# Local attention's score sums: two streamed columns a product in place of 128

## The chip, the cores and the metric

The kernel runs on one core of one Trainium2 chip. The metric is the device time of one execution in microseconds (us); lower is better. The time before is the median of three runs.

## The reference

Two blocks of a small transformer run over `x` of 8 sequences (B) by 256 tokens (T) by 128 features. The change touches only the first stage of the first block, a local attention with 16 heads of 64 features, in which each token looks at four keys: one made from the conditioning vector of its sequence, and those of the token before it, of itself and of the token after it.

```python
q = (x @ WQ_w + WQ_b).reshape(Bx, Lx, nh, d)
k = (x @ WK_w + WK_b).reshape(Bx, Lx, nh, d)
ak = (ax @ WK_w + WK_b).reshape(Bx, 1, nh, d)
av = (ax @ WV_w + WV_b).reshape(Bx, 1, nh, d)
...
K = jnp.concatenate([akb, k_shift], axis=3)
V = jnp.concatenate([avb, k_shift], axis=3)
scores = jnp.einsum('blhd,blhjd->blhj', q, K) / jnp.sqrt(jnp.float32(d))
alphas = jax.nn.softmax(scores, axis=-1)
att = jnp.einsum('blhj,blhjd->blhd', alphas, V).reshape(Bx, Lx, nh * d)
return att @ WO_w + WO_b
```

After it come a linear attention, a recurrent scan with a routed feed-forward layer, a second scan with a differential attention, and a top-2 mixture of experts. They are not changed.

## The kernel before

`program` runs its stages one after the other, each in a `Block` of its own, and the next one's instructions start only when all engines have left the block before. `local_attention` is the second stage, after the small `setup`.

Features lie on the 128 partitions, tokens in the free dimension. A chunk `c` of 128 features is two heads, so there are 8 chunks; the 2048 tokens are cut into two halves of 1024. One half and one chunk is a unit `u`, and there are 16. For each unit:

- `project(u, i)` (TensorE, L280) makes queries and keys in five pieces: two of 512 query columns, two of 512 key columns, and one of 8. ScalarE (`keep_projections`, L367 and L370) copies each into `qb` and `kb`.
- `products(u)` (VectorE, L434 and L437) multiplies the query with each of the four keys, element by element, into `prod`: four operations of 128 x 1024.
- `scores(u, i)` (TensorE, L292) sums these products over the 64 features of each head. For token block `i` of 128 tokens (eight in a unit, `HB`) and key `j` (four, `J`), the 128 x 128 tile of `prod` is the stationary operand and a selector `headsel` is the streamed one. `headsel` has two columns that are not zero, ones in the first 64 partitions and ones in the last 64. All 32 sums of a unit are one accumulation group over the whole 128-column tile `sc`: a window of `headsel` is shifted so that its two columns of ones fall on columns `2k` and `2k + 1`, and the other 126 columns add zero.
- `softmax(u)` (VectorE, L447 to L472, with one exponential on ScalarE) reads the 64 used columns of `sc` and splits the probabilities into three bf16 parts; `turn_probs` (TensorE, L303) turns them over, ScalarE copies them (`keep_turned`, L381).
- `spread_probs(u, i)` (TensorE, L314) spreads each probability over the 64 features of its head, eight tiles of 512 columns; `terms` (VectorE, L482 and L486) multiplies each with its value into `term`, and `attended` (L493 and L497) adds them up to `att`.
- `project_out` (TensorE, L322) multiplies with the output weights and accumulates over chunks.

The order on each engine is written out by hand. In turn `u` of the main loop TensorE issues `scores(u + 1, 0)`, then seven times `scores(u + 1, i + 1)` followed by `spread_probs(u, i)`, and then `project(u + 3, 0)`, the eighth `spread_probs`, `project(u + 3, 1)`, `project_out(u - 1, 1)`, the three key pieces, `project_out(u, 0)` and `turn_probs(u + 1)`. VectorE issues `products(u + 2)`, `attended(u - 1, 1)`, six `terms`, `softmax(u + 1)`, `attended(u, 0)` and two `terms`. `bc`, the target of a spread, has two buffers, so a spread waits for the term two before it. In the last three turns there is nothing left to project.

In fp32 one `nc.tensor.matmul` of the program is two pairs of a weight load and a matmul in the trace, so the 512 score sums are 1024 pairs, 64 for a unit.

Of the kernel before, what the change touches and what calls it, by code (L numbers as in the profile page):

```python
# [33 lines left out]
P = 128  # L34
# [3 lines left out]
HEADS, HD = 16, 64  # L38
# [133 lines left out]
def local_attention(nc, n, a, yB, wq, wk, wv, wo, wqkv, wout):  # L172

    HALF = TOK // 2
    HB = HALF // P
# [3 lines left out]
    J = 4  # L179
    with ExitStack() as local:  # L180
        def sb(name, shape, dt=F32):
            return local.enter_context(nc.sbuf_tensor(name, shape, dt))
# [5 lines left out]

        headsel = sb("headsel", [P, 2 * P])
        pick = sb("pick", [24, J, 2, HD], BF16)
        akT, avT = sb("akT", [P, NC, B]), sb("avT", [P, NC, B])
        qb = [sb(f"qb{i}", [P, HALF]) for i in range(4)]
# [1 line left out]
        prod = [sb(f"prod{i}", [P, J, HALF]) for i in range(2)]  # L196
# [10 lines left out]
        sc = local.enter_context(nc.psum_tensor("sc", [P, P // (2 * J), J, 2], F32))  # L207
# [13 lines left out]
        def pieces(u):  # L221
            h, c = divmod(u, NC)
            t0 = h * HALF
            k0 = 0 if h == 0 else t0 - SH
            return ([("q", t0, 0, 512), ("q", t0 + 512, 512, 512)]
                    + [("k", k0, SH, 512), ("k", k0 + 512, SH + 512, 512), ("k", k0 + 1024, SH + 1024, SH)])
# [6 lines left out]
        with nc.Block() as block:  # L233

            @block.sync
            def _(sp):
                sp.dma_start(wqkv[:, :], a["L0_attn_Wqkv"]).then_inc(n.load_linear, 16)
                sp.dma_start(wout[:, :, :], a["L0_attn_Wout"].rearrange("(c p) d -> p c d", p=P)).then_inc(n.load_linear, 16)
                for i, key in enumerate(("L0_cond2_W_ir", "L0_cond2_W_iz", "L0_cond2_W_in",
                                         "L0_cond2_W_hr", "L0_cond2_W_hz", "L0_cond2_W_hn")):  # L240
                    sp.dma_start(n.gru_w[:, i, :], a[key]).then_inc(n.load_later, 16)
                for i, key in enumerate(("L0_cond2_b_hn", "L0_cond2_b_ir", "L0_cond2_b_iz", "L0_cond2_b_in")):
                    sp.dma_start(n.gru_b[:, i, :], a[key].rearrange("(r d) -> r d", r=1)).then_inc(n.load_later, 16)
                sp.dma_start(n.b_l1[:, :], a["L1_cond_b"].rearrange("(r d) -> r d", r=1)).then_inc(n.load_later, 16)
                for dst, key in ((n.l1w, "L1_cond_W"), (n.wq12, "L1_attn_w_q12"), (n.wk12, "L1_attn_w_k12"),
                                 (n.wv1, "L1_attn_w_v"), (n.wmod, "L1_cond2_weight"), (n.b2, "L0_ffn_b2")):
                    sp.dma_start(dst[:, :], a[key]).then_inc(n.load_later, 16)
# [10 lines left out]
            @block.tensor  # L258
            def _(pe):
                pe.wait_ge(n.load_local, 64)  # L260

                for i, w in enumerate((wk, wv)):
                    for c in range(NC):
                        mm = nc.tensor.matmul(pj[i][:, B * c:B * c + B], w[:, P * c:P * c + P], n.condT,
                                              start=True, stop=True)
                    mm.then_inc(cond_proj, 1)
                pe.wait_ge(cond_kept, 2)
                pe.wait_ge(const_done, 2)
                pe.wait_ge(const_a, 4)

                def project(u, i):
                    if u >= UNITS:
                        return
                    c = u % NC
                    kind, src, _, width = pieces(u)[i]
                    w = wq if kind == "q" else wk
                    g = 5 * u + i
                    if g >= 2:
                        pe.wait_ge(proj_kept, g - 1)
                    nc.tensor.matmul(pj[g % 2][:, 0:width], w[:, P * c:P * c + P], n.xT[:, src:src + width],  # L280
                                     start=True, stop=True).then_inc(proj_done, 1)

                def scores(u, i):
                    if u >= UNITS:
                        return
                    if u >= 1 and i == 0:
                        pe.wait_ge(soft, 9 * u - 7)
                    if i == 0:
                        pe.wait_ge(prod_v, 4 * (u + 1))
                    for j in range(J):  # L290
                        k = J * i + j
                        mm = nc.tensor.matmul(sc[:, :, :, :].rearrange("p i j h -> p (i j h)"),  # L292
                                              prod[u % 2][:, j, P * i:P * i + P], headsel[:, P - 2 * k:2 * P - 2 * k],
                                              start=(k == 0), stop=(k == HB * J - 1))
                    if i == HB - 1:
                        mm.then_inc(score_done, 1)

                def turn_probs(u):
                    pe.wait_ge(parts_done, u + 1)
                    if u >= 1:  # L300
                        pe.wait_ge(turned_kept, u)
                    for i in range(HB):
                        mm = nc.tensor.transpose(tr[:, P * i:P * i + P],  # L303
                                                 parts[u % 2][:, i, :, :].rearrange("p k r -> p (k r)"), n.identb[:, :])
                    mm.then_inc(turned, 1)

                def spread_probs(u, i):
                    if i == 0:
                        pe.wait_ge(turned_kept, u + 1)
                    m, j = divmod(i, J)  # L310
                    g = 2 * J * u + i
                    if g >= 2:
                        pe.wait_ge(term_done, g - 1)
                    nc.tensor.matmul(bc[g % 2][:, :], pick[:, j, :, :].rearrange("r h d -> r (h d)"),  # L314
                                     probT[u % 2][:, 512 * m:512 * m + 512], start=True, stop=True).then_inc(spread, 1)

                def project_out(u, m):
                    h, c = divmod(u, NC)
                    if c == 0 and h == 1:
                        pe.wait_ge(y_kept, m + 1)  # L320
                    pe.wait_ge(att_done, 2 * u + m + 1)
                    nc.tensor.matmul(y_ps[m][:, :], wo[:, c, :], att[m][:, :], start=(c == 0),  # L322
                                     stop=(c == NC - 1)).then_inc(y_part, 1)

                for u in range(2):
                    for i in range(5):
                        project(u, i)
                for i in range(HB):
                    scores(0, i)
                for i in range(5):  # L330
                    project(2, i)
                turn_probs(0)


                for u in range(UNITS):
                    scores(u + 1, 0)
                    for i in range(HB - 1):
                        scores(u + 1, i + 1)
                        spread_probs(u, i)
                    project(u + 3, 0)  # L340
                    spread_probs(u, HB - 1)
                    project(u + 3, 1)
                    if u >= 1:
                        project_out(u - 1, 1)
                    for i in range(2, 5):
                        project(u + 3, i)
                    project_out(u, 0)
                    if u + 1 < UNITS:
                        turn_probs(u + 1)
                project_out(UNITS - 1, 1)  # L350
# [57 lines left out]
            def _(dve):  # L408
# [2 lines left out]
                nc.vector.memset(headsel[:, :], 0.0).then_inc(const_done, 1)  # L411
                dve.wait_ge(const_done, 1)
                for h in range(2):
                    nc.vector.memset(headsel[HD * h:HD * h + HD, P + h:P + h + 1], 1.0)

                for i in range(4):
                    nc.vector.memset(kb[i][:, 0:SH], 0.0)
# [1762 lines left out]
def program(nc, a, out):  # L2180
    with ExitStack() as ctx:
        n = allocate(nc, ctx)
        with ExitStack() as mid:
            yB = mid.enter_context(nc.sbuf_tensor("yB", [P, TOK], F32))
            wqkv = mid.enter_context(nc.sbuf_tensor("wqkv", [P, 3 * INNER], F32))
            wout = mid.enter_context(nc.sbuf_tensor("wout", [P, NC, D], F32))
            with ExitStack() as early:
                wq, wk, wv = (early.enter_context(nc.sbuf_tensor(k, [P, INNER], F32)) for k in ("wq", "wk", "wv"))
                wo = early.enter_context(nc.sbuf_tensor("wo", [P, NC, D], F32))
                setup(nc, n, a, wq, wk, wv, wo)  # L2190
                local_attention(nc, n, a, yB, wq, wk, wv, wo, wqkv, wout)
            linear_attention(nc, n, yB, wqkv, wout)
# [38 lines left out]
```

## Time and profile before

| | |
|---|---|
| three runs | 1698.83, 1699.10, 1703.48 us; median 1699.1 us |
| profiled execution | 1703.39 us in all, of which the span from the first instruction to the last is 1701.6 us |
| busy share over the span | TensorE 92%, VectorE 49%, ScalarE 39%, GpSimd 6% |
| granted TensorE clock, mean | 0.942 of full speed |
| local attention with `setup` | from 0 to about 371 us of the span |

Times inside the profile count from the start of the span. The profiled execution is 4.3 us longer than the median of the three runs, so a difference that is worked out inside it is added to both. The granted clock is given as a share of 2.4 GHz: 1.00 is that, and 0.50 is the other level, 1.2 GHz.

### The profile page before, as it was taken

The numbers are of one execution on the slowest core, as the hardware profiler recorded it, in microseconds if no ns is written. First come the engines' busy times: TensorE is split into PE (matmuls) and PEld (weight loads), VectorE is DVE, ScalarE is ACT, GpSimd is POOL, SyncE is SP. The second block draws the span as 40 slices with busy tenths as digits, with TensorE's granted clock in tenths as the row PEclk, the third lists the DMA queues.
The fourth block names the chain that finished last, engine by engine and source line by source line (L and its number), as shares of the span: only waits on it lengthen the run. The fifth ranks groups of instructions, "written<-read, shape, count | busy, mean of one in ns | idle before, by whom it ended". The sixth has DMA issues, their size and how long they took to land. (4 is left out here: it accounts for less than half of the span.)

```text
span 1701.6 us, 32009 instructions
## 1 busy us (share of the span) xinstructions
PE 1564.6 (92%) x11861; PEld 1250.0 (73%) x11862; DVE 827.5 (49%) x2926; ACT 662.9 (39%) x2449; POOL 94.7 (6%) x135
## 2 busy tenths in 40 slices
PE   7999989879999899999999999879999999866995
PEld 5666555537777799999999999638888888753663
DVE  2777668755445334444444444473333333565223
ACT  3211112125555145555555455314344434523442
POOL 0000000000000000000000000010000000003662
PEclk9988889889999999999999999859999999967998
DMA  4000000000000300000000000010000000001113
GB/s 146 1 1 1 0 1 1 1 0 1 1 1 1 100 1 2 2 1 2 2 2 1 2 2 1 1 31 21 20 26 20 27 14 2 1 1 47 41 43 92
DMA packets 27731, 28.05 MB, mean 16 GB/s; under 512 B 2293, under 2 KB 22234, under 8 KB 27450
## 3 DMA queue, kind: packets, MB, share of 16 engines
q1 hardware_dynamic: 20970, 16.70, 3.4%
q0 software_dynamic: 2496, 5.12, 1.0%
q10 hardware_dynamic: 4112, 4.19, 0.8%
q8 instruction: 96, 1.57, 0.4%
q14 instruction: 57, 0.47, 0.1%
HBM read 21.35 MB, written 4.65 MB: 15 GB/s over the span
## 5 line engine op out<-in xcount | busy, mean ns | idle before, releaser
L1457 PE MATMUL spare<-identb 128*128 128x128 bf16 x3166 | 218.2, 219 | 0.0
L1457 PEld LDWEIGHTS spare<-identb 128*128 128x128 bf16 x3166 | 201.7, 103 | 4.3
L292 PE MATMUL sc<-headsel,prod 128*128 128x128 f32 x1024 | 164.6, 315 | 0.7 <-DVE prod L437 0.7
L292 PEld LDWEIGHTS sc<-headsel,prod 128*128 128x128 f32 x1024 | 142.6, 218 | 26.7 <-issue 24.3
L1055 DVE TENSOR_TENSOR_SCAN narg<-rz,pre_n 128x16 f32<-128x16 f32 x256 | 47.9, 187 | 219.9 <-PE pre_n L952 218.9
L990 ACT ACTIVATE ghid<-gh_ps,cols 128x128 f32<-128x128 f32 x512 | 144.3, 366 | 12.9 <-PE gh_ps L891 12.7
L891 PE MATMUL gh_ps<-hist,w 128*128 128x128 f32 x1024 | 137.5, 275 | 0.6 <-ACT ghid L990 0.6
L900 PE MATMUL gy_ps<-w2e,ghid 128*128 128x128 f32 x1024 | 136.8, 276 | 0.6
L900 PEld LDWEIGHTS gy_ps<-w2e,ghid 128*128 128x128 f32 x1024 | 124.4, 191 | 3.0 <-issue 3.0
L891 PEld LDWEIGHTS gh_ps<-hist,w 128*128 128x128 f32 x1024 | 126.0, 188 | 0.8 <-DVE hist L1063 0.8
L952 PE MATMUL pre_r<-hist,gru_w 128*128 128x128 f32 x512 | 118.1, 312 | 0.7 <-DVE hist L1063 0.5
L1508 DVE TENSOR_TENSOR_SCAN targ<-gates,pairs 128x16 f32<-128x16 f32 x256 | 49.1, 192 | 141.4 <-ACT gates L1467 141.4
L976 ACT ACTIVATE rz<-pre_r 128x8 f32<-128x8 f32 x256 | 45.5, 178 | 182.6 <-PE pre_r L952 179.9
L1427 PEld LDWEIGHTS s_pre<-s,wT 128*128 128x128 f32 x512 | 76.9, 189 | 41.6 <-ACT s L1470 41.0
L1427 PE MATMUL s_pre<-s,wT 128*128 128x8 f32 x512 | 97.9, 263 | 2.9 <-ACT s L1470 1.1
L952 PE MATMUL pre_z<-hist,gru_w 128*128 128x128 f32 x512 | 100.0, 276 | 0.0
L952 PE MATMUL pre_n<-hist,gru_w 128*128 128x128 f32 x512 | 99.8, 276 | 0.0
L1505 DVE TENSOR_SCALAR pairs<-s,leak 128x8 f32<-128x8 f32 x256 | 59.6, 233 | 70.7 <-ACT s L1470 70.5
L952 PEld LDWEIGHTS pre_r<-hist,gru_w 128*128 128x128 f32 x512 | 77.1, 190 | 15.8 <-DVE hist L1063 1.0
L1467 ACT ACTIVATE gates<-s_pre 128x8 f32<-128x8 f32 x256 | 45.5, 178 | 108.0 <-PE s_pre L1427 108.0
L1470 ACT ACTIVATE s<-targ 128x8 f32<-128x8 f32 x256 | 53.4, 209 | 84.7 <-DVE targ L1508 84.7
L486 DVE TENSOR_TENSOR term<-bc,kb 128x512 f32<-128x512 f32 x96 | 63.3, 686 | 34.6 <-PE bc L314 34.4
(374 smaller groups left out, 2664.1 us busy)
## 6 DMA issues: line engine op xcount, KB each, us to landing
w<-in_L_ffn_W SPq DMA_DIRECT2D x1, 2048.0 KB, 9.6
raw<-in_L_ffn_wg SPq DMA_DIRECT2D x8, 256.0 KB, 2.9
raw<-in_L_ffn_wu SPq DMA_DIRECT2D x8, 256.0 KB, 2.8
raw<-in_L_ffn_wd SPq DMA_DIRECT2D x8, 256.0 KB, 2.7
wqkv<-in_L_attn_Wqkv SPq DMA_DIRECT2D x1, 1536.0 KB, 6.4
mrow<-mt SPq DMA_DIRECT2D x4, 256.0 KB, 2.4
y_top<-yrow SPq DMA_DIRECT2D x4, 256.0 KB, 5.4
y_next<-yrow ACTq DMA_DIRECT2D x4, 256.0 KB, 6.1
```

Source lines behind the costliest of these rows:

```text
L292: mm = nc.tensor.matmul(sc[:, :, :, :].rearrange("p i j h -> p (i j h)"), prod[u % 2][:, j, P * i:P * i + P], headsel[:, P - 2 * k:2 * P - ...
L486: nc.vector.tensor_tensor(term[s % 2][:, j, :], bc[g % 2][:, :], key(u, j, 512 * m, 512), ALU.mult).then_inc(term_done, 1)
L891: mm = nc.tensor.matmul(h_ps[:, f, :], w1[:, e, P * f:P * f + P], tokens(g), start=True, stop=True)
L900: mm = nc.tensor.matmul(y_ps, hid[v % 2][:, f, :], w2[:, e, f, :], start=(f == 0), stop=(f == NF - 1))
L952: nc.tensor.matmul(out, n.gru_w[:, i, :], h, start=False, stop=True, skip_group_check=True).then_inc(ready, 1)
L990: nc.scalar.activation(hid[v % 2][:, f, :], h_ps[:, f, :], ACT.Relu, bias=n.cols[:, at:at + 1]).then_inc(h_done, 1)
L1055: V.tensor_tensor_scan(narg[p][:, :], rz[p][:, 0:16], n_slot(s), 0.0, ALU.mult, ALU.add).then_inc(narg_done, 1)
L1427: nc.tensor.matmul(pre[s // G % 2][:, at:at + B], wT[:, 0, :], s2[:, 8 * s:8 * s + B], start=False, stop=True, skip_group_check=True).then ...
L1457: nc.tensor.matmul(spare[:, 0:P], n.identb[:, :], n.identb[:, :], start=True, stop=True)
L1470: nc.scalar.activation(s2[:, 8 * s + 8:8 * s + 16], second(targ[s % 2][:, :]), ACT.Tanh).then_inc(state, 1)
L1505: nc.vector.tensor_scalar(second(pair), s2[:, 8 * s:8 * s + 8], leak[:, 0:1], None, ALU.mult).then_inc(leaked, 1)
L1508: nc.vector.tensor_tensor_scan(targ[s % 2][:, :], gates[s % 2][:, :], pair, 0.0, ALU.mult, ALU.add).then_inc(arg_done, 1)
```

## The change

Each score sum becomes a matmul of its own. It streams two columns and writes two columns of `sc`, and it starts and stops its accumulation itself. The selector shrinks to two columns. The weight loads, their number and their order, the waits and the semaphores stay as they are.

```diff
-        headsel = sb("headsel", [P, 2 * P])
+        headsel = sb("headsel", [P, 2])
...
                     for j in range(J):
-                        k = J * i + j
-                        mm = nc.tensor.matmul(sc[:, :, :, :].rearrange("p i j h -> p (i j h)"),
-                                              prod[u % 2][:, j, P * i:P * i + P], headsel[:, P - 2 * k:2 * P - 2 * k],
-                                              start=(k == 0), stop=(k == HB * J - 1))
+                        mm = nc.tensor.matmul(sc[:, i, j, :], prod[u % 2][:, j, P * i:P * i + P], headsel[:, :],
+                                              start=True, stop=True)
                     if i == HB - 1:
                         mm.then_inc(score_done, 1)
...
                 for h in range(2):
-                    nc.vector.memset(headsel[HD * h:HD * h + HD, P + h:P + h + 1], 1.0)
+                    nc.vector.memset(headsel[HD * h:HD * h + HD, h:h + 1], 1.0)
```

## Rows read from the trace of the kernel before

**Rows 1.** The profile's page, second part: granted clock in 40 slices of the span

```profile
PEclk9988889889999999999999999859999999967998
```

**Rows 2.** The page's costliest groups: the score sums

```profile
L292 PE MATMUL sc<-headsel,prod 128*128 128x128 f32 x1024 | 164.6, 315 | 0.7 <-DVE prod L437 0.7
```

**Rows 3.** Timeline, turn 11: start, us, engine, what; in brackets idle before

```profile
278.14 1.22 DVE L434 TENSOR_TENSOR prod<-qb,akT 128x1024 f32<-128x1024 f32 x1 [0.29 <-ACT kb L370]
...
278.97 2.05 PE L292 MATMUL sc<-headsel,prod 128*128 128x128 f32 x16
...
285.29 0.38 PE L314 MATMUL bc<-probT,pick 24*128 24x512 bf16 x1 [1.46 <-DVE term L482]
...
286.70 0.39 PE L314 MATMUL bc<-probT,pick 24*128 24x512 bf16 x1
...
290.91 0.39 PE L314 MATMUL bc<-probT,pick 24*128 24x512 bf16 x1
...
297.22 1.22 DVE L434 TENSOR_TENSOR prod<-qb,akT 128x1024 f32<-128x1024 f32 x1 [0.29 <-ACT kb L370]
```

**Rows 4.** Timeline, ScalarE, just after the starts of turns 0, 13 and 14

```profile
43.79 1.01 ACT L381 ACTIVATE probT<-tr 24x1024 bf16<-24x1024 bf16 x1
...
317.23 1.01 ACT L381 ACTIVATE probT<-tr 24x1024 bf16<-24x1024 bf16 x1 [0.97 <-PE tr L303]
...
338.55 1.01 ACT L381 ACTIVATE probT<-tr 24x1024 bf16<-24x1024 bf16 x1 [7.06 <-PE tr L303]
```

**Rows 5.** Windows: length, busy us (count) of PE, PEld, DVE, ACT, POOL, PE clock, DMA share, GB/s

```profile
154.00:160.00 6.00, 6.00 (x24) 4.68 (x24) 1.70 (x3) 0.00 (x0) 0.00 (x0) 0.50 0.00 0
...
280.00:300.00 20.00, 18.54 (x104) 11.92 (x102) 16.46 (x28) 4.26 (x8) 0.00 (x0) 1.00 0.00 1
```

**Rows 6.** Timeline, TensorE: turns 5, 13 and 14

```profile
155.51 0.60 PE L314 MATMUL bc<-probT,pick 24*128 24x512 bf16 x1
...
158.05 0.60 PE L314 MATMUL bc<-probT,pick 24*128 24x512 bf16 x1
...
330.61 0.60 PE L314 MATMUL bc<-probT,pick 24*128 24x512 bf16 x2
...
338.44 3.39 PE L292 MATMUL sc<-headsel,prod 128*128 128x128 f32 x16
```

**Rows 7.** Timeline, the stretch up to 40 us

```profile
16.74 3.53 PEld L264 LDWEIGHTS pj<-cols,wv 128*128 128x128 f32 x16
...
20.82 3.47 PE L280 MATMUL pj<-xT,wq 128*128 128x512 f32 x4 [0.45 <-DVE avT L424]
...
31.86 7.22 PEld L292 LDWEIGHTS sc<-headsel,prod 128*128 128x128 f32 x64 [0.80 <-DVE prod L437]
...
39.01 0.30 PEld L280 LDWEIGHTS pj<-xT,wq 128*128 128x128 f32 x2
```

**Rows 8.** Timeline, last stage: router products of 8 columns, then transposes of 128

```profile
1524.13 5.49 PEld L1845 LDWEIGHTS bank_a<-cols,mB 128*128 128x128 f32 x32 [2.10 <-DVE mB L1992]
...
1529.36 1.76 PEld L1836 LDWEIGHTS xt_ps<-ident,mB 128*128 128x128 f32 x8
```

**Rows 9.** Windows of the same stage, columns as in Rows 5

```profile
1516.40:1522.00 5.60, 5.59 (x7) 2.50 (x8) 4.05 (x7) 0.00 (x0) 1.11 (x9) 0.50 0.01 1
...
1524.10:1525.50 1.40, 1.37 (x13) 1.37 (x13) 0.00 (x0) 0.00 (x0) 0.00 (x0) 1.00 0.00 0
1526.00:1529.30 3.30, 3.30 (x17) 3.30 (x17) 0.00 (x0) 0.00 (x0) 0.00 (x0) 0.50 0.00 0
1529.40:1532.40 3.00, 3.00 (x15) 2.63 (x16) 2.37 (x9) 1.20 (x2) 0.00 (x0) 0.50 0.04 11
1533.00:1534.00 1.00, 0.00 (x1) 0.00 (x0) 0.96 (x4) 0.98 (x3) 0.00 (x0) 1.00 1.07 286
```

**Rows 10.** Timeline, routing stage: eight bf16 products that stream one column

```profile
1102.37 0.29 PEld L1235 LDWEIGHTS r_sums<-r_ones,r_gt 128*128 128x128 bf16 x8 [0.73 <-DVE r_gt L1279]
...
1102.59 0.10 PEld L1238 LDWEIGHTS r_sums<-r_zeros,r_ones 128*128 128x128 bf16 x1
```

## The prediction

> **What bounds the kernel now.** I read the page's slices first, then the costliest groups, then the timeline of one turn of local attention, then the windows for the granted clock. The stages run one after the other, so what local attention gains or loses goes into the total one to one. Its score sums are the second largest group of the page: 1024 matmuls, mean 315 ns [rows 2]. The slices show that the clock is not at full speed in this stage: it is at 8 tenths in several of the first slices [rows 1].
>
> In the timeline of turn 11, which ran wholly at full clock, a turn lasts 297.22 - 278.14 = 19.08 us, and neither engine bounds it alone [rows 3]. VectorE starts its four products at 278.14; TensorE starts 16 pairs of score sums at 278.97, and at the third spread it stands for 1.46 us, until VectorE has released a `bc` buffer. That spread goes at 285.29, 6.32 us after the first score sum, and this interval is VectorE's. From there to the seventh spread at 290.91 TensorE sets the pace: four groups of one spread and eight score pairs, 1.41 us each. Then come query pieces, the last spread, output products, key pieces, and with them the copies that VectorE's next products wait for. So only four of a turn's eight groups of score pairs lie on the path that sets its length.
>
> The other thing to see is the clock. From the start of turn 0 to the start of turn 13 it takes 317.23 - 43.79 = 273.4 us [rows 4], 21.0 us for each of 13 turns, and not 19.08. The missing 25 us are stretches at half clock, like 154 to 160 us, in which the granted clock is 0.50 though TensorE is busy throughout [rows 5]. In such a stretch a group takes 158.05 - 155.51 = 2.54 us in place of 1.41, and 16 pairs take 3.39 us [rows 6].
>
> **The change part by part.** *The selector.* A memset becomes smaller, before VectorE's wait for the first projections. Nothing on the path: 0.
>
> *The streaming of 126 columns that add zero.* What does a pair cost now, and after? At full clock 64 pairs take 39.01 - 31.86 = 7.15 us, 112 ns each [rows 7]. A pair is a load of a 128 x 128 fp32 tile and a matmul, and loads overlap with matmuls. The nearest rows for a narrow product are the router's: the same fp32 tile as stationary operand, eight columns streamed. At granted clock 1.00 there are 13 of them in the window's 1.37 busy us, 105 ns each [rows 9]; at half clock 17 in 3.30 us, 194 ns, against 3.39 / 16 = 212 ns for the wide pair [rows 6, 9]. Windows count a cut instruction too, so these are low ends; all 32 take 1529.36 - 1524.13 = 5.23 us [rows 8], which is 13 at 112 ns and 19 at 199 ns. The start of the kernel has 16 more narrow pairs in 3.53 us, 220 ns each, at half speed by the next row, where a matmul of 512 columns takes 3.47 / 4 = 0.87 us [rows 7]. So the load sets a pair's time, narrow or wide, and the change takes next to nothing from it. The other end is the cheapest narrow product of the trace: eight bf16 ones of one column in 1102.59 - 1102.37 = 0.22 us, 28 ns each [rows 10]. Their stationary tile is bf16; the fp32 rows are nearer, and I take a saving of nothing per pair. What is saved is the end of each group, where the last wide product still streams while the spread behind it is loaded: at most one matmul, 0.1 us at full clock and 0.2 at half. I take half of that: a group at half clock costs 2.45 us, not 2.54.
>
> The Trainium skill has two rules here ("TensorE: Matmul & The Clock Gate"). "Back-to-back issue gap" makes the time fall with the streamed columns, to some 25 ns for a few of them; by this alone 64 pairs would shrink from 7.2 to an estimated 1.6 us. "LDWEIGHTS (loading the stationary operand)" makes the load go with the 128 columns of the stationary tile, an estimated 107 ns, and by this nothing is saved. The fp32 rows side with the second.
>
> *What the clock does.* This is the term that decides. In the last stage the clock is at 1.00 when the router's narrow products begin at 1524.13; it is still 1.00 up to 1525.5 and 0.50 from 1526 on, with TensorE and its weight loads busy for 3.30 of 3.30 us, and it stays there until 128-column transposes have run for over 3 us [rows 8, 9]. At the start of the kernel over 3 us of the same kind of product leave the speed at half as well [rows 7]. Weight loads and narrow products do not hold the clock in these rows. After the change the score sums are such products, and they fill most of the time from a turn's start to its seventh spread. Already now the clock is lost for a while in some turns, with wide products [rows 4, 5]. I expect it to fall in each turn's score part, and to come back in the part with the 512-column projections.
>
> *A turn after the change.* Score part: at the start the clock may still be full. If it falls 1.6 to 3.3 us in, TensorE has lost what the 1.46 us wait used to hold, and the third spread still goes about when VectorE releases it, at 6.32 us. Four groups at half clock follow: 4 x 2.45 = 9.8 us, against 5.6 now. The score part is 16.1 us in place of 290.91 - 278.97 = 11.9. Projection part: the turn's other 19.08 - 11.9 = 7.1 us of TensorE work at full clock. How long it runs at half, I bound by two rows: the transposes needed over 3.0 us, and 512-column products 5.6 us or a little more [rows 9]. I take the middle, 4.6 us, in which it does 2.3 us of its work: 9.4 us. A turn is 16.1 + 9.4 = 25.5 us.
>
> *The sum.* Turns 0 to 12: 13 x 25.5 = 331.5 us against 273.4: +58. Turn 13 has no projections: its score part was 330.61 - 317.12 = 13.5 us (its first score sum comes 0.11 us before the copy of rows 4) and becomes 16.1: +3. Turn 14 already begins at half clock, with 16 pairs in 3.39 us [rows 6], and is not held up by VectorE's products; its six groups go from 1.41 to 2.45 us: +6. The 64 pairs of unit 0, at 31.86, have full clock for some 3 us and then 0.21 us a pair in place of 0.112 [rows 6, 7]: 11 us against 7.15, and 2 more before the clock is back: +6. Together +73. The profiled execution would take 1703.4 + 73 = 1776 us, and the median 1699.1 + 73 = 1772 us.
>
> **The rivals.**
>
> *The clock holds (faster, 10%).* If weight loads count as work, TensorE is as busy as before and the clock behaves as now, or better. For it: TensorE's row is busy throughout, and the window from 280 to 300 us has the present pattern at 1.00 [rows 5]. Against it: 3.30 us of unbroken loads at 0.50 [rows 9]. Then only the group ends are saved: 0.1 us x 4 groups x 16 turns = 6 us at most, and should the present half-clock stretches vanish too, another 25. I price it at 1693, at best 1668. It decides if the clock stays at 1.00 in the score part for more than about 8 of 13 turns. The Trainium skill supports it ("TensorE: Matmul & The Clock Gate", "HAM oscillation"): it lays the loss of the clock to idle gaps of TensorE, and the change adds none. By that rule the time would be the 1693 above; the router's rows disagree.
>
> *The pair gets cheap (faster, 4%).* If a narrow fp32 pair cost 28 ns, TensorE would no longer bound even at half clock, and VectorE would: it is busy 16.46 of 20 us [rows 5], so 15.7 of 19.08, and with its wait for ScalarE a turn would be some 16.5. 13 x (21.0 - 16.5) = 58 us less: 1641. The router's 32 narrow pairs in 5.23 us speak against it.
>
> *The clock stays down (slower still, 12%).* If the projections of a turn do not bring the clock back before the next score part, all is at half: 3.4 + 6 x 2.45 = 18.1 us up to the seventh spread, and 7.1 us of TensorE work, most of which doubles, some 13: 31 us a turn, 13 x 10 = 130 more, with the 15 of the other turns 1844. Against it: clocks came back in 3 to 6 us of dense streaming, and the projection part at half clock lasts twice that.
>
> *Half as bad (slower, 6%).* The clock falls in about half of the turns, or late in each: half of the 73 us, 1736.
>
> **How the numbers follow.** The forecast, that the clock falls in each score part and comes back in each projection part, gets 68%. Its own range: with 3.2 us at half in the projections and groups of 2.35 us a turn is 24.4 us, 1756; with 5.9 us at half and a clock that falls after 1.6 us, so that the third spread is 1 us late, 27.2 us, and 1798. The range for all reaches from the half-bad case to the lower part of the all-half case: 1732 to 1840. It leaves out the two faster rivals, 14%, and about half of the all-half one. A measurement of this kernel tells about 0.3%, 5 us, from no change. Faster by more than that: 11% (both faster rivals, less the part in which only a few us are saved). Within 0.3%: 3%. Slower: 86%.
>
> **What the profile after would show.** The granted clock of 20 to 375 us at 0.6 to 0.75; it falls in the score part and rises in the key pieces of nearly every turn. Starts of turns some 25.5 us apart. No 1.46 us wait at the third spread, or a short one. 64 pairs of unit 0 still over 7 us. Stages after local attention the same length. The prediction is wrong if score pairs come at under 80 ns, or if the clock stays at 1.00 through score parts.

## The result, and the profile after

The changed kernel takes 1776.9 us (median of four runs, 1776.35 to 1777.74) against 1699.0 us before: slower by a factor of 1.0461, 95% interval 1.0428 to 1.0494. The forecast was 1772 us. The profiled execution took 1776.35 us, its span 1774.6 us.

From the page of the kernel after, the clock slices and the two groups of the score sums, to be held against [rows 1, 2]:

```profile
PEclk7666566565999999999999999967999999976998
...
L291 PEld LDWEIGHTS sc<-headsel,prod 128*128 128x128 f32 x1024 | 190.5, 281 | 36.8 <-issue 34.5
...
L291 PE MATMUL sc<-headsel,prod 128*128 128x2 f32 x1024 | 199.7, 320 | 0.7 <-DVE prod L435 0.7
```

A matmul of two columns has a mean of 320 ns, where one of 128 columns had 315 [rows 2]. These means mix matmuls at full and at half clock, and more of the narrow ones ran at half. The shortest, at full clock, took 251 ns where the shortest wide one took 274: streaming 64 times less made the instruction hardly shorter. And the first ten slices, in which local attention lies, went from mostly 8 and 9 tenths of the clock to 5, 6 and 7.

Turn 3 of the kernel after on the timeline, TensorE (start, us, engine, what), against turn 11 of before in [rows 3]. The last line belongs to turn 4:

```profile
124.24 1.95 PE L291 MATMUL sc<-headsel,prod 128*128 128x2 f32 x16
126.11 0.39 PE L312 MATMUL bc<-probT,pick 24*128 24x512 bf16 x1
126.43 1.05 PE L291 MATMUL sc<-headsel,prod 128*128 128x2 f32 x8
127.42 0.39 PE L312 MATMUL bc<-probT,pick 24*128 24x512 bf16 x1
127.73 1.80 PE L291 MATMUL sc<-headsel,prod 128*128 128x2 f32 x8
130.56 0.60 PE L312 MATMUL bc<-probT,pick 24*128 24x512 bf16 x1 [1.02 <-DVE term L480]
131.09 1.87 PE L291 MATMUL sc<-headsel,prod 128*128 128x2 f32 x8
132.89 0.60 PE L312 MATMUL bc<-probT,pick 24*128 24x512 bf16 x1
...
139.89 0.60 PE L312 MATMUL bc<-probT,pick 24*128 24x512 bf16 x1
140.43 2.08 PE L280 MATMUL pj<-xT,wq 128*128 128x512 f32 x2
...
149.36 1.83 PE L291 MATMUL sc<-headsel,prod 128*128 128x2 f32 x15
```

The first 16 pairs take 1.87 us and the first group 1.31 us, from 126.11 to 127.42, where a wide group took 1.41: that is all that the narrower stream gains at full clock, and it is gained where TensorE waits anyway. Then, just before 128 us, the clock falls: the next eight pairs take 1.80 us. TensorE had not stood still once in this turn up to then; its wait of 1.02 us comes after the fall. The third spread still goes 6.32 us after the first score sum, when VectorE releases it; four groups of 2.33 us follow; the query pieces of 512 columns start at half clock; and the next turn begins 25.1 us after this one did. The windows of the same stretch (length, busy us and count of PE, PEld, DVE, ACT, POOL, clock, DMA share, GB/s):

```profile
128.00:144.00 16.00, 14.97 (x50) 10.19 (x50) 9.14 (x20) 0.94 (x2) 0.00 (x0) 0.50 0.00 1
145.00:151.00 6.00, 6.00 (x34) 3.43 (x32) 3.37 (x5) 3.23 (x5) 0.00 (x0) 1.00 0.00 0
152.00:171.50 19.50, 19.45 (x60) 12.82 (x60) 12.14 (x24) 1.63 (x3) 0.00 (x0) 0.50 0.00 1
172.50:178.50 6.00, 6.00 (x40) 3.91 (x38) 3.77 (x4) 2.55 (x4) 0.00 (x0) 1.00 0.01 1
```

From 152 to 171.5 us TensorE is busy for 19.45 of 19.50 us and has half its clock. ScalarE's copies behind the starts of turns 0, 13, 14 and 15, and the last copy of the stage, show where the time went; they answer to [rows 4], and behind them, by itself, stands the last copy of the kernel before:

```profile
48.44 1.01 ACT L379 ACTIVATE probT<-tr 24x1024 bf16<-24x1024 bf16 x1
...
383.92 1.01 ACT L379 ACTIVATE probT<-tr 24x1024 bf16<-24x1024 bf16 x1 [0.97 <-PE tr L301]
...
407.40 1.01 ACT L379 ACTIVATE probT<-tr 24x1024 bf16<-24x1024 bf16 x1 [7.06 <-PE tr L301]
...
429.94 1.01 ACT L379 ACTIVATE probT<-tr 24x1024 bf16<-24x1024 bf16 x1 [7.05 <-PE tr L301]
...
442.93 1.12 ACT L387 ACTIVATE yB<-y_ps,cols 128x512 f32<-128x512 f32 x1 [1.66 <-PE y_ps L320]
```

```profile
369.76 1.12 ACT L389 ACTIVATE yB<-y_ps,cols 128x512 f32<-128x512 f32 x1 [0.71 <-PE y_ps L322]
```

Thirteen turns take 383.92 - 48.44 = 335.5 us against 273.4. The last copy came at 369.76 in the kernel before, so the stage ends 73.2 us later, and what is left of the span is 1774.6 - 442.9 = 1331.7 us against 1701.6 - 369.8 = 1331.8 us. All of the loss is in `setup` and local attention.

The two profiled executions are 1776.35 - 1703.39 = 73.0 us apart, the medians 1776.9 - 1699.0 = 77.9 us. The four runs of the kernel before spread over 10.6 us (1692.93 to 1703.48) and its profiled one lay near the upper end; the four of the changed kernel spread over 1.4 us.

### The profile page after: what moved, and what is told of

Read it like the earlier page. It is cut to its first block and busy times, and to the rows that moved or that the text cites. A ratio compares the mean times of both kernels' runs of the same rounds, so it can differ in the third digit from the quotient of the medians.

```text
span 1774.6 us, 32010 instructions
## 1 busy us (share of the span) xinstructions
PE 1653.9 (93%) x11862; PEld 1309.7 (74%) x11862; DVE 827.3 (47%) x2926; ACT 665.4 (37%) x2449; POOL 94.7 (5%) x135
## 5 line engine op out<-in xcount | busy, mean ns | idle before, releaser
L291 PEld LDWEIGHTS sc<-headsel,prod 128*128 128x128 f32 x1024 | 190.5, 281 | 36.8 <-issue 34.5
L291 PE MATMUL sc<-headsel,prod 128*128 128x2 f32 x1024 | 199.7, 320 | 0.7 <-DVE prod L435 0.7
L950 PEld LDWEIGHTS pre_r<-hist,gru_w 128*128 128x128 f32 x512 | 77.1, 190 | 15.8 <-DVE hist L1061 1.0
L373 ACT ACTIVATE s_exp<-s_sh 128x64 f32<-128x64 f32 x16 | 4.1, 256 | 223.1 <-DVE s_sh L447 223.1
```

The lines of the kernel that those rows point to most:

```text
L291: mm = nc.tensor.matmul(sc[:, i, j, :], prod[u % 2][:, j, P * i:P * i + P], headsel[:, :], start=True, stop=True)
L950: nc.tensor.matmul(out, n.gru_w[:, i, :], h, start=False, stop=True, skip_group_check=True).then_inc(ready, 1)
```

## Experiments

The theory: the weight load sets the time of a score pair, whatever it streams; and the granted clock follows how much TensorE streams, so that the 126 columns of zeros were what held it up. The rivals: the 32 separate accumulation groups of a unit cost the time (A), or the clock goes with idle gaps of TensorE alone (B). E3, E4, E5, E8 and E9 have two runs each, E2, E6 and E7 four, E1 eight. The median of the kernel before was 1700.6 us beside the first four kernels, 1699.9 us beside the next four, 1700.4 us beside the last.

**E1, the flags alone.** 128 columns, but each product starts and stops its own group. It overwrites the scores of the products before it, so the result is wrong; the work of the engines is the same.

```diff
-                                              start=(k == 0), stop=(k == HB * J - 1))
+                                              start=True, stop=True)
```

> The kernel before with its 128 streamed columns, but each score product starts and stops its own accumulation, as in the change; every product then overwrites the whole tile, so that only the last product's two scores survive: the scores are changed, the work of each engine is not. Theory (the streamed columns hold the clock, the weight load sets a pair's time): same as before, 1699 us within 6 us, granted clock from 20 to 375 us near 0.89. Rival A (the 32 separate accumulation groups cost the time): near 1777 us.

Measured 1698.9 us, ratio 0.9996 (0.9972 to 1.002), granted clock 0.92 from 20 to 375 us. Rival A is out: what is left is the width. A product writes as many columns of `sc` as it streams, in every run here, so streaming and writing are not told apart.

**E2, E3, E4, E5, the width.** The same sums with a stream of `w` columns, in accumulation groups that cover `w` columns of `sc`. All give the same scores.

```diff
-                        mm = nc.tensor.matmul(sc[:, :, :, :].rearrange("p i j h -> p (i j h)"),
-                                              prod[u % 2][:, j, P * i:P * i + P], headsel[:, P - 2 * k:2 * P - 2 * k],
-                                              start=(k == 0), stop=(k == HB * J - 1))
+                        at, kk = w * (2 * k // w), k % (w // 2)
+                        mm = nc.tensor.matmul(sc[:, :, :, :].rearrange("p i j h -> p (i j h)")[:, at:at + w],
+                                              prod[u % 2][:, j, P * i:P * i + P], headsel[:, P - 2 * kk:P - 2 * kk + w],
+                                              start=(kk == 0), stop=(kk == w // 2 - 1))
```

With 96 columns it is one group over columns 0 to 95.

> Score sums stream 64 columns, in one accumulation group over the 64 columns of sc that are used. Theory: a pair costs the same 105 to 113 ns at full clock, a group some 0.05 us less; the clock is lost in more turns than before, but not in all: 1715 to 1760 us. Rival A (accumulation groups): one group as before, so 1699 us. Rival B (the clock is lost to idle gaps of TensorE alone, and width does not matter): 1693 us.

> Score sums stream 32 columns, two accumulation groups a unit. Theory: the clock falls in each turn's score part as with two columns, 1765 to 1780 us. Rival A (accumulation groups): 1/16 of the change's groups, so near 1704 us. Rival B: 1693 us.

> Score sums stream 8 columns, eight accumulation groups a unit, one for each token block. Theory: as the change, 1777 us within 4 us, half-clock groups of 2.33 us. Rival A: a quarter of the way, 1718 us.

> Score sums stream 96 columns, one accumulation group. With 64 columns the time was that of the change (1777 us), with 128 that of the kernel before (1701 us). Theory (how much TensorE streams decides on the clock): somewhere between, 1715 to 1765 us, with a granted clock from 20 to 375 us between the 0.70 of 64 columns and the 0.89 of 128. Rival (the clock has nothing to do with width but with the unused half of the tile sc being written): 96 columns write it too, so 1701 us.

| columns streamed | us | ratio (interval) | clock, 20 to 375 us |
|---|---|---|---|
| 2 (the change) | 1776.9 | 1.0461 (1.0428 to 1.0494) | 0.64 |
| 8 | 1776.6 | 1.0449 (1.0428 to 1.0470) | 0.65 |
| 32 | 1776.8 | 1.0450 (1.0429 to 1.0471) | 0.67 |
| 64 | 1777.0 | 1.0445 (1.0426 to 1.0463) | 0.70 |
| 96 | 1740.1 | 1.0234 (1.0176 to 1.0292) | 0.78 |
| 128, own groups (E1) | 1698.9 | 0.9996 (0.9972 to 1.0020) | 0.92 |
| 128 (before) | 1699.0 | | 0.89 |

Eight and 32 columns came as expected, 96 too, though its two runs lie 15.8 us apart (1732.18 and 1747.93). 64 did not: I had expected part of the loss, 1715 to 1760 us, and it was all of it. The timeline of E2, turn 10, shows why its higher mean clock bought nothing:

```profile
313.68 0.39 PE L316 MATMUL bc<-probT,pick 24*128 24x512 bf16 x1
314.00 1.10 PE L294 MATMUL sc<-headsel,prod 128*128 128x64 f32 x8
316.72 0.38 PE L316 MATMUL bc<-probT,pick 24*128 24x512 bf16 x1 [1.62 <-DVE term L484]
317.04 1.72 PE L294 MATMUL sc<-headsel,prod 128*128 128x64 f32 x8
318.69 0.60 PE L316 MATMUL bc<-probT,pick 24*128 24x512 bf16 x1
...
321.12 0.60 PE L316 MATMUL bc<-probT,pick 24*128 24x512 bf16 x1
...
325.99 0.60 PE L316 MATMUL bc<-probT,pick 24*128 24x512 bf16 x1
```

```profile
316.50:317.00 0.50, 0.28 (x1) 0.09 (x1) 0.50 (x2) 0.00 (x0) 0.00 (x0) 1.00 0.00 0
317.00:317.50 0.50, 0.50 (x5) 0.47 (x4) 0.50 (x2) 0.00 (x0) 0.00 (x0) 0.84 0.00 0
317.50:318.00 0.50, 0.50 (x4) 0.50 (x3) 0.36 (x1) 0.00 (x0) 0.00 (x0) 0.50 0.00 0
```

The clock falls a little later in the turn, but the time kept is mostly the time before the third spread, which only lengthens the wait (1.62 us here). Of the four groups on the path the first is still partly at full clock (318.69 - 316.72 = 1.97 us); the next takes 321.12 - 318.69 = 2.43 us, where the change's take 2.33. All four take 325.99 - 316.72 = 9.27 us, the change's 139.89 - 130.56 = 9.33. The program's order and its waits are the same in E2 to E5, so the width decides between them, and a stream of half the columns loses the clock in each of turns 0 to 12 as well.

Rival B, idle gaps alone, is out by the place of the fall. In windows of half a microsecond over turns 0 to 12, the changed kernel's clock falls some 2.3 to 4.4 us after the first score sum of a turn, before TensorE has waited at all; that of the kernel before falls in nine of them, some 6.4 to 8.4 us in, behind the wait. With 64 columns it falls once the wait has begun in 11 of the 13 turns, as in the three windows above. Whether 64 columns would keep the clock without the wait was not tried.

**E6, E7, the wait filled.** If the kernel before loses its clock in the 1.46 us wait ahead of the third spread, products by 128 columns of zeros in that wait should keep it. They add zero to the accumulation, so the result is the reference's.

```diff
                         scores(u + 1, i + 1)
+                        if i == 2 and u + 1 < UNITS:
+                            for _ in range(3):    # E7: 6
+                                nc.tensor.matmul(sc[:, :, :, :].rearrange("p i j h -> p (i j h)"),
+                                                 prod[(u + 1) % 2][:, 0, 0:P], headsel[:, 0:P], start=False, stop=False)
                         spread_probs(u, i)
```

> The kernel before with three more products by 128 columns of zeros in the score group's accumulation, ahead of each turn's third spread, where TensorE stands for 1.46 us; they add zero. They take 0.7 us of that wait at full clock. Theory (the half-clock stretches of the kernel before come from this wait): fewer falls, 1680 to 1697 us. Rival (the falls have another cause, or the added work delays the path): 1701 to 1710 us.

> The same with six added products, 1.35 us of the 1.46 us wait at full clock. Theory: the clock stays at 1.00 in turns 0 to 12, which then take 19.1 us each: 25 us less than before, 1672 to 1682 us. Rival (another cause): no fewer falls, and 2.5 us more in each half-clock turn, 1705 to 1725 us.

E6 took 1679.9 us, ratio 0.9881 (0.9861 to 0.9901); E7 1681.2 us, ratio 0.9882 (0.9858 to 0.9905). E6 thus came just below the time expected for it, E7 within. Windows from the start of turn 0 into turn 13, first E6, then E7:

```profile
44.00:310.00 266.00, 249.99 (x1378) 161.56 (x1378) 213.42 (x359) 57.20 (x95) 0.00 (x0) 1.00 0.00 1
```

```profile
44.00:312.00 268.00, 260.07 (x1471) 171.53 (x1470) 214.14 (x360) 57.89 (x97) 0.00 (x0) 1.00 0.00 1
```

The clock is 1.00 throughout, 0.91 in the kernel before from 44 to 317 us, its turns 0 to 12. Those turns take 250.3 us in E6, 23.1 less. In E6 the third spreads of two turns running stand 19.08 us apart, the full-clock turn of [rows 3], though TensorE waits for less:

```profile
142.61 0.83 PE L341 MATMUL sc<-headsel,prod 128*128 128x128 f32 x6
144.24 0.38 PE L314 MATMUL bc<-probT,pick 24*128 24x512 bf16 x1 [0.79 <-DVE term L486]
...
161.69 0.83 PE L341 MATMUL sc<-headsel,prod 128*128 128x128 f32 x6
163.32 0.38 PE L314 MATMUL bc<-probT,pick 24*128 24x512 bf16 x1 [0.79 <-DVE term L486]
```

Dead work in a wait made the kernel 1.2% faster than the faster of the two versions under study. E6 and E7 cannot be told apart.

**E8, E9, dead work in the changed kernel.** Three or six bf16 matmuls of 448 columns ahead of seven of the eight groups, by a constant tile of ones, into an unused part of the bank of `sc`.

```diff
+                    for _ in range(3 if i else 0):    # E9: 6
+                        nc.tensor.matmul(sc[:, :, :, :].rearrange("p i j h -> p (i j h)")[:, 64:512],
+                                         n.identb[:, :], dense[:, 0:448], start=True, stop=True)
                     for j in range(J):
```

> The changed kernel with two columns, plus three bf16 matmuls of 448 columns ahead of each of seven of the eight groups of a unit, into an unused part of the bank of sc: dead work, 0.24 us each at full clock, 5 us a turn. Theory: if this streaming is enough to hold the clock, a turn is 6.6 + 4 x 2.0 + 7.1 = 21.8 us, and the kernel is faster than the change although it does more, near 1725 us; if it is not enough, the added work runs at half clock and the time is 1830 to 1870 us. Rival (a pair of two columns is slow in itself, whatever the clock): about 1777 us plus 13 turns x 4 groups x 0.7 us, 1815 us, with the clock back at 1.00.

> As the kernel with three dead bf16 matmuls a group, which kept half clock in the score part and took 1859 us, with six a group. Theory (the clock goes by how much TensorE streams): twice the dead work holds the clock; a group is 1.3 + 6 x 0.2 = 2.5 us, a turn 1.9 + 1.2 + 2 x 2.5 + 4 x 2.5 + 7.1 = 25 us, and the time falls below that with three, to 1780 to 1810 us, with the clock of 20 to 375 us above 0.9. Rival (a product of two columns pulls the clock down whatever streams beside it): the added three matmuls run at half clock as well, 28 us a unit at 0.4 us for each of 21, and the time is about 1859 + 16 x 8.4 x 0.8, near 1960 us.

E8 took 1858.9 us, ratio 1.0933 (1.0902 to 1.0965), clock 0.64: the other branch of the theory's expectation, not enough to hold the clock. E9, with twice the dead work, took 1813.1 us (1804.05 and 1822.17), ratio 1.0654 (1.0520 to 1.0788), clock 0.88; a little above the expected 1780 to 1810 us and below the expected clock of over 0.9, because five of turns 0 to 12 still lose it. The end of a group in E8, then in E9:

```profile
155.47 0.60 PE L317 MATMUL bc<-probT,pick 24*128 24x512 bf16 x1
156.01 1.30 PE L293 MATMUL sc<-dense,identb 128*128 128x448 bf16 x3
157.10 1.71 PE L296 MATMUL sc<-headsel,prod 128*128 128x2 f32 x8
158.74 0.60 PE L317 MATMUL bc<-probT,pick 24*128 24x512 bf16 x1
```

```profile
153.10 0.38 PE L317 MATMUL bc<-probT,pick 24*128 24x512 bf16 x1
153.42 1.31 PE L293 MATMUL sc<-dense,identb 128*128 128x448 bf16 x6
154.56 0.95 PE L296 MATMUL sc<-headsel,prod 128*128 128x2 f32 x8
155.44 0.38 PE L317 MATMUL bc<-probT,pick 24*128 24x512 bf16 x1
```

With six dead matmuls a group takes 2.34 us, with three 3.27 us. The same eight two-column pairs take 0.95 us in the one and 1.71 us in the other. This rules out the rival that a product of two columns pulls the clock down whatever runs beside it, and the one that it is slow in itself. In E9 the dead work also fills the wait at the third spread, so E9 alone does not part the stream from the wait; the place of the fall in the changed kernel does.

## Why the prediction was right

*What sets a pair's time: right.* At full clock a group went from 1.41 to 1.31 us and at half from 2.54 to 2.33. A pair still costs a load; only the ends of the groups became shorter. I had taken half of the possible 0.2 us at half clock, and it was all of it. The Trainium skill's "LDWEIGHTS (loading the stationary operand)" ("TensorE: Matmul & The Clock Gate") makes a load of 128 columns an estimated 107 ns; the trace agrees at full clock, with 16 pairs in 1.87 us, 117 ns each. Its "Back-to-back issue gap" has a floor of about 25 ns for a matmul by itself, which the prediction set against this, and says that in a stream of loads and matmuls both set the spacing. The trace sides with the second statement.

*What the clock does: right,* and in every turn. It was forecast at 0.6 to 0.75 from 20 to 375 us and is 0.64. It falls some 2.3 to 4.4 us after a turn's first score sum, forecast 1.6 to 3.3. It is back some 4.3 to 6.9 us after the first 512-column piece starts; counted from the seventh spread that is 5 us in turn 3 and 7 us in turn 4, where 4.6 was forecast, 5.9 at the most. E1 to E5, E8 and E9 show that the width of the stream is the cause. The Trainium skill's idle-gap rule ("TensorE: Matmul & The Clock Gate", "HAM oscillation") does not give this: the change lost its clock ahead of its wait. E6 and E7, where filling a wait kept the clock, go in that rule's direction, for a wait shorter than those the section describes.

*The sum: right in total, with errors that cancel.*

| stretch | forecast | measured |
|---|---|---|
| before the score sums of unit 0 | 0 | -1.8 |
| unit 0 and what follows up to turn 0 | +6 | +6.4 |
| turns 0 to 12 | +58 | +62.0 |
| turn 13 | +3 | +2.2 |
| turn 14 | +6 | +3.0 |
| turn 15 | 0 | +1.4 |
| together | +73 | +73.2 |

A turn was forecast at 16.1 + 9.4 = 25.5 us. Turn 3 has 139.89 - 124.24 = 15.7 us, the cheaper groups, and 149.36 - 139.89 = 9.5 us, together 25.1. About every other turn takes 26.2, such as turn 4:

```profile
155.68 0.60 PE L312 MATMUL bc<-probT,pick 24*128 24x512 bf16 x1
...
165.01 0.60 PE L312 MATMUL bc<-probT,pick 24*128 24x512 bf16 x1
...
175.56 1.95 PE L291 MATMUL sc<-headsel,prod 128*128 128x2 f32 x16
```

Its clock falls 1.2 us earlier in the turn, and that costs nothing: the third spread goes 155.68 - 149.36 = 6.32 us in, the seventh 15.65 us in, just as in turn 3. The difference is in the projection part, 175.56 - 165.01 = 10.6 us, where the clock stays down for 2 us more. So the score part was forecast 0.4 us too long and the projection part on average 0.5 us too short, and the two cancel: without turn 8 the mean of the turns is 25.5 us.

The 4 us that turns 0 to 12 took beyond the forecast are all in turn 8. It takes 281.31 - 251.94 = 29.4 us, with two waits of TensorE, of 1.81 and 1.18 us, that the others do not have. The kernel before has them too; its turn 8 took 25.6 us:

```profile
276.16 2.29 PE L280 MATMUL pj<-xT,wk 128*128 128x512 f32 x6 [1.81 <-ACT qb L365]
279.63 1.10 PE L320 MATMUL y_ps<-att,wo 128*128 128x512 f32 x2 [1.18 <-DVE att L495]
```

```profile
232.48 2.29 PE L280 MATMUL pj<-xT,wk 128*128 128x512 f32 x6 [1.81 <-ACT qb L367]
235.96 1.09 PE L322 MATMUL y_ps<-att,wo 128*128 128x512 f32 x2 [1.19 <-DVE att L497]
```

The forecast counted turn 8 like the rest after the change, and not before it. Turn 14 was mis-sized too:

```profile
407.29 2.14 PE L291 MATMUL sc<-headsel,prod 128*128 128x2 f32 x16
409.37 0.39 PE L312 MATMUL bc<-probT,pick 24*128 24x512 bf16 x1
...
410.67 0.39 PE L312 MATMUL bc<-probT,pick 24*128 24x512 bf16 x1
...
412.67 0.60 PE L312 MATMUL bc<-probT,pick 24*128 24x512 bf16 x1
```

I took its 16 first pairs as at half clock before and after. In the changed kernel the clock came back as they began (409.37 - 407.29 = 2.1 us against 3.39), which gains 1.3 us, and the first two of the six groups kept all or part of it (1.30 and 2.00 us, where 2.45 was forecast), 1.6 us more. The -1.8 us ahead of unit 0 is from `setup`: the first 16 of its narrow pairs took 1.8 us in the profile of the change and 3.4 us in the one before.

That the total met the forecast to 0.2 us is luck in part. The forecast of the profiled execution, 1776 us, was met as well (1776.35); that of the median, 1772, was 4.9 us short, because it took over the 4.3 us by which the profiled execution of the kernel before was longer than its median. The changed kernel has no such distance.

*The rivals.* The clock did not hold, the pair did not get cheap, the clock fell in all of turns 0 to 12 and not in half of them, and it did not stay down through the projections. The 25 us that I named as what the present half-clock stretches cost were nearly right: E6 got 23.1 us back in turns 0 to 12 and 20 us by the medians, without the change. Some 3 us of the 25 were the two waits of turn 8 and had nothing to do with the clock; in E6, at full clock, that turn still takes 22.5 us.

## What to carry to other kernels

Where each product needs a new stationary tile, count the loads: in these fp32 pairs a narrower stream behind the same loads saved next to nothing. Columns that add zero are not free to take away, if they are what keeps TensorE streaming; look at the granted clock of the stretches whose streams would shrink, and find a place in the same trace where narrow products run alone. A short wait inside a dense loop may cost more by the clock than by its length; zero products in it are cheap to try.

## What had not been expected

A stream of 64 columns lost as much time as one of 2, and 96 columns about half: 1777.0, 1776.9 and 1740.1 us. Width shows in how long the clock stays down more than in how often it falls: with 96 columns it fell in ten of turns 0 to 12 and stayed down for 10 to 17 us, with 128 in nine, for 3 to 7 us (one profile of each). The streamed columns that hold the clock may be all zeros but for two. And half clock outlasted the wide stream too: in the kernel before, TensorE ran wide score sums without a gap from 154 to 160 us at 0.50 [rows 5]. What brings the clock back in one such stretch sooner than in another was not tried.
